# First-layer projection of a graph-attention block by one level of Strassen's scheme, logit rows kept in the result's last head

## The chip, the cores and the metric

One core of a Trainium2 chip runs the whole program as one launch. The metric is the device time of an execution in microseconds (us), less is better. Five engines work side by side, each through its own list of instructions in order: TensorE (PE, matrix products into PSUM; its weight loads are shown apart as PEld), VectorE (DVE), ScalarE (ACT), GpSimd (POOL) and SyncE (SP), which here issues most of the transfers (DMA). They wait for each other by semaphores: `wait_ge(sem, n)` stops an engine until `sem` has reached n, `then_inc` counts it up when an instruction is done.

## The reference, cut to what matters

The program is one transformer-like block for 1250 nodes of width 768: a layer norm, a two-layer graph attention network, a mixing layer, and a mixture of experts. The change touches the first graph layer:

```python
h = (x @ W).reshape(N, H, C)              # N 1250, x 768 wide, H 4 heads of C 512
al_s = einsum('nhc,hc->nh', h, a_src)
al_d = einsum('nhc,hc->nh', h, a_dst)
e = leaky_relu(al_s[src] + al_d[dst], 0.2)
m = segment_max(e, dst)                   # over the edges into a node
ex = exp(e - m[dst])
alpha = ex / (segment_sum(ex, dst)[dst] + 1e-16)
out = segment_sum(h[src] * alpha[:, :, None], dst)
```

All of it is float32. The edges have been counted earlier into a dense table of 1250 x 1250 counts, so that sums over edges become products with that table.

## The kernel before, in words

The phases follow each other with a barrier in between; the change lies in `first_layer_phase`, which computes three things at once.

**The projection** h = xn W. The normed input lies turned in SBUF as `xnT`, 6 blocks of 128 of its 768 features (KD = 6) by 1250 nodes. Nodes go in 10 tiles of 125 (NT, P), and W comes in 4 parts of 512 columns (C1), one for each head, into two buffers `w` in turn. A unit is one head and one tile: 6 float32 products of 125 nodes by 512 columns, summed up in one of two PSUM banks `G` (line 972), and copied by ScalarE into `h` (line 929). There are 40 units, head by head. Unit g waits until the copy of unit g - 2 is done.

**The attention logits**: 8 rows (4 heads, source and target side) from `wa`, as 3 x 6 products at the phase's start (line 978). ScalarE copies them to `alT` (line 951), SP stores them to DRAM and loads the four source rows back, spread over all partitions, as `rows` (line 862). TensorE also turns them (line 984) for `al`.

**The maxima**: for every tile t of target nodes, its counts are loaded (`ct`, lines 101 and 102), VectorE adds the self loop (line 898, function `loop`), ScalarE makes a mask of them (line 937), and VectorE takes for each of 4 heads the largest logit among the neighbours (line 914, 40 in all). TensorE turns the counts in ten blocks into a set of three PSUM banks `T` (line 996), ScalarE copies them to `co` (line 945), and GpSimd issues the stores of masks and counts for later phases. There are two sets `T`.

The order of each engine is written out by hand. TensorE: logits, unit 0, the turn of the logits, then units with the turn of tile t behind unit 3 + 2t, and the turn of the maxima (line 1004) behind unit 30. ScalarE copies each unit, and behind unit 3 + 2t the counts and then the mask of tile t + 2. VectorE has nothing to do with the products: it only does self loops and maxima. SP loads the counts of tile t when tile t - 2 has been turned and masked, the weights of head 2 behind the counts of tile 5, and those of head 3 last.

The next phase, `gat1_phase`, multiplies attention weights with `h` in halves of 256 columns (line 1188, into four banks `Z`).

Of the kernel before, what the change touches and what calls it, by code (L numbers as in the profile page):

```python
# [9 lines left out]
I32 = mybir.dt.int32  # L10
# [798 lines left out]
def first_layer_phase(nc, cx, W1, xnT, wa, ident, al, alT_dram, ct_dram, c_dram, mask_dram, mT_dram, h):  # L809
# [3 lines left out]
    MASK0, MAX_UNIT = 3, 30  # L813
    UNITS = H1 * NT
    J = 2 * H1
    gemm, h_evac, rows_done, rows_copied, al_turned, al_stored = (
        cx.sem("first_" + s) for s in ("gemm", "h_evac", "rows_done", "rows_copied", "al_turned", "al_stored"))
# [7 lines left out]
    dve_step = cx.sem("mask_step")  # L825
    with ExitStack() as st:
        w = [sb(nc, st, f"gnn_w1_{b}", [128, KD, C1]) for b in range(2)]
        alT = sb(nc, st, "logit_alT", [J, N])
# [3 lines left out]
        rows = sb(nc, st, "mask_rows", [128, H1, N])  # L832
# [4 lines left out]
        mT = sb(nc, st, "mask_mT", [H1, N])  # L837
        G = [pb(nc, st, f"first_G{b}", [P, C1]) for b in range(2)]
        T = [[pb(nc, st, f"mask_T{b}{j}", [128, 512]) for j in range(3)] for b in range(2)]
        width = [4, 4, 2]  # L840
        tiles = lambda bank, j, rows: bank[rows, 0:width[j] * P].rearrange("p (t d) -> p t d", d=P)
        block = st.enter_context(nc.Block())

        @block.sync
        def _(sp):
# [13 lines left out]
            sp.dma_start(alT_dram, alT[:]).then_inc(al_stored, 16)  # L859
# [3 lines left out]
            for t in range(2, NT):  # L863
                sp.wait_ge(turned, t - 1)
# [8 lines left out]
            sp.dma_start(mT_dram, mT[:]).then_inc(m_stored, 16)  # L873
# [3 lines left out]
        def _(pool):  # L877
            pool.memset(large[:], BIG).then_inc(consts, 1)
            pool.memset(h[:, :, :, C1:C1 + 1], 1.0)
            for t in range(NT):  # L880
# [4 lines left out]
                pool.dma_start(c_dram[t, :, :], co[b][:].rearrange("p t d -> p (t d)")).then_inc(c_stores[b], 16)  # L885
            for b in range(2):
                pool.wait_ge(mask_stores[b], 16 * (NT // 2))
                pool.wait_ge(c_stores[b], 16 * (NT // 2))

        @block.vector  # L890
        def _(dve):
# [7 lines left out]

            loop(0)  # L900
            loop(1)
            dve.wait_ge(al_turned, 1)
            step(dve.tensor_copy(al[:], T[1][0][0:P, 0:NT * J].rearrange("p (t j) -> p t j", j=J)))
            dve.wait_ge(rows_loaded, 64)
            for t in range(NT):
                b = t % 2
                if 1 <= t < NT - 1:
                    loop(t + 1)
                dve.wait_ge(masked, t + 1)
                for hd in range(H1):  # L910
                    n = H1 * t + hd
                    if n >= 1:
                        dve.wait_ge(maxed, n)
                    dve.tensor_tensor_reduce(out=junk[:], in0=rows[0:P, hd, :], in1=mk[b][:], scale=1.0,
                                             scalar=-3.0e38, op0=ALU.subtract, op1=ALU.max,
                                             accum_out=big[:, t, hd:hd + 1]).then_inc(maxed, 1)
            dve.wait_ge(maxed, H1 * NT)
            step(dve.tensor_tensor(big[:], big[:], al[:, :, H1:2 * H1], ALU.add))
            dve.scalar_tensor_tensor(m[:], big[:], SLOPE, big[:], ALU.mult, ALU.max).then_inc(m_ready, 1)
            for j in range(3):  # L920
                dve.wait_ge(m_turned, j + 1)
                dve.tensor_copy(mT[:, 4 * j * P:(4 * j + width[j]) * P], T[0][j][0:H1, 0:width[j] * P]
# [1410 lines left out]
```

## Time and profile before

| | us |
|---|---|
| median of 3 executions | 2211.65 (2207.43 to 2214.65) |
| the profiled execution, its own time | 2213.6 |
| its span | 2211.8 |
| TensorE busy in the span | 2084.3 (94%) |
| VectorE, ScalarE, GpSimd busy | 1107.5, 456.1, 199.3 |
| first-layer phase, from its first load to the next phase's first | 648.0 to 884.1 |

Times in the trace are counted from the start of the span. A busy time is the sum over an engine's instructions, without overlaps; an idle time is what stands before an instruction, with the one that ended it. A float32 product stands in the trace as two MATMUL rows, each with its own weight load, and a MATMUL row is longer than its distance to the next, since the end of one lies over the start of the next. The granted clock (PEclk) is a share of 2.4 GHz; it has the levels 1.00 and 0.50.

### The profile page before, as it was taken

To read this page: it belongs to the slowest core of one execution; us is meant where nothing else is said; L and a number is where in the kernel's file an instruction comes from. 1 tells how busy PE (TensorE), PEld (TensorE's weight loads), DVE (VectorE), ACT (ScalarE), POOL (GpSimd) and SP (SyncE) were. 2 spreads that over 40 slices of the span, in tenths; PEclk is the share of its full clock that TensorE was granted. 3 is DMA by queue.
4 is the path that set the end of the run, shared out by engine and by line. 5 is a ranking of instruction groups with operands and counts; after the bars stand their busy time and mean duration, and the time that the engine had idled before them with its cause. 6 is when DMAs were issued, how large, how long until landed. Compare 5 with 4: busy or idle time off the path is not lost. (4 is left out here: it accounts for less than half of the span.)

```text
span 2211.8 us, 32691 instructions
## 1 busy us (share of the span) xinstructions
PE 2084.3 (94%) x9768; PEld 1435.0 (65%) x9769; DVE 1107.5 (50%) x2517; ACT 456.1 (21%) x818; POOL 199.3 (9%) x187
## 2 busy tenths in 40 slices
PE   5999999999989999799999989998997999999997
PEld 3666566666644444688888745554664777777775
DVE  5766447662554510788888600306854343333343
ACT  2222221222002311122222200002432222222221
POOL 0000000000000000000000000001003233333232
PEclk9999999998999999899999989998995999999999
DMA  7000220002644510443333264424404888899654
GB/s 247 15 16 17 87 101 15 16 18 77 204 130 138 171 57 1 154 122 98 120 96 98 66 224 152 157 103 111 153 29 177 250 229 247 244 291 278 190 128 78
DMA packets 80954, 282.32 MB, mean 128 GB/s; under 512 B 11562, under 2 KB 32098, under 8 KB 71267
## 3 DMA queue, kind: packets, MB, share of 16 engines
q1 hardware_dynamic: 59858, 216.48, 29.2%
q0 software_dynamic: 14048, 51.06, 10.0%
q10 hardware_dynamic: 6960, 13.62, 1.8%
q8 instruction: 53, 0.87, 0.2%
q14 instruction: 35, 0.28, 0.0%
HBM read 222.26 MB, written 58.87 MB: 127 GB/s over the span
## 5 line engine op out<-in xcount | busy, mean ns | idle before, releaser
L1188 PE MATMUL gat_Z<-h,gat_wt 125*125 125x256 f32 (+1 forms) x1600 | 355.0, 381 | 17.8 <-DVE gat_wt L1104 17.8
L1188 PEld LDWEIGHTS gat_Z<-h,gat_wt 125*125 125x125 f32 x1600 | 298.2, 188 | 63.6 <-DVE gat_wt L1104 18.6
L732 PE MATMUL mix_G<-mix_w,xnT 128*125 128x384 f32 x720 | 243.8, 489 | 0.0
L1335 PE MATMUL gat2p_Y<-w_and_experts,gat2p_hT 128*125 128x386 f32 (+1 forms) x640 | 209.8, 490 | 10.2 <-DMA w_and_experts<-in_L_gnn_W 10.2
L972 PE MATMUL first_G<-gnn_w,xnT 128*125 128x512 f32 x480 | 208.3, 593 | 0.0
L732 PEld LDWEIGHTS mix_G<-mix_w,xnT 128*125 128x125 f32 x720 | 133.6, 190 | 85.6 <-issue 3.4
L1335 PEld LDWEIGHTS gat2p_Y<-w_and_experts,gat2p_hT 128*125 128x125 f32 x640 | 120.2, 188 | 98.5 <-issue 12.6
L972 PEld LDWEIGHTS first_G<-gnn_w,xnT 128*125 128x125 f32 x480 | 89.1, 188 | 110.4 <-issue 110.3
L1822 PE MATMUL gat_Z<-h,gat_wt 125*125 125x385 f32 (+1 forms) x400 | 135.7, 496 | 12.6 <-DVE gat_wt L1556 12.6
L1822 PEld LDWEIGHTS gat_Z<-h,gat_wt 125*125 125x125 f32 x400 | 74.8, 190 | 66.7 <-DVE gat_wt L1556 13.3
L639 DVE SCALAR_TENSOR_TENSOR mix_count_A<-count_ikey,count_off,keyT 128x512 f32 x120 | 90.2, 752 | 55.1 <-issue 46.9
L2059 DVE TENSOR_SCALAR ex_idS<-ex_ids 128x1 int32 x52 | 8.0, 154 | 214.1 <-DMA out_rows<-ex_y,ex_idS 214.1
L2147 PE MATMUL ex_PH<-ex_xT,w_and_experts 128*128 128x128 f32 x936 | 113.8, 282 | 1.5
L645 DVE TENSOR_SCALAR mix_count_B<-count_islo,sloT 128x314 f16 x480 | 112.1, 299 | 0.0
L2147 PE MATMUL ex_PH<-ex_xT,ex_w 128*128 128x128 f32 x936 | 111.0, 277 | 0.9 <-issue 0.3
L2147 PEld LDWEIGHTS ex_PH<-ex_xT,w_and_experts 128*128 128x128 f32 x936 | 109.2, 196 | 2.5 <-issue 2.2
L2157 PE MATMUL ex_PY<-ex_w,ex_hT 128*128 128x384 f32 x312 | 107.2, 493 | 0.9 <-ACT ex_hT L2088 0.9
L2157 PE MATMUL ex_PY<-w_and_experts,ex_hT 128*128 128x384 f32 x312 | 107.5, 494 | 0.5 <-ACT ex_hT L2088 0.5
L2147 PEld LDWEIGHTS ex_PH<-ex_xT,ex_w 128*128 128x128 f32 x936 | 106.5, 192 | 1.4 <-issue 1.4
L2004 POOL DMA_INDIRECT out_rows<-ex_y,ex_idS x52 | 82.6, 1588 | 271.3 <-DVE ex_y L2061 226.4
L2029 DVE SCALAR_TENSOR_TENSOR ex_Q<-posm,offs,ex_iota 125x1280 bf16<-125x1280 f32 x54 | 83.8, 1552 | 39.0 <-issue 39.0
L780 PE MATMUL mix_count_S<-mix_count_B,mix_count_A 128*128 x480 | 86.4, 297 | 5.2 <-issue 2.7
(310 smaller groups left out, 2490.7 us busy)
## 6 DMA issues: line engine op xcount, KB each, us to landing
w_and_experts<-in_L_ffn_W SPq DMA_DIRECT2D x32, 1152.0 KB
ex_w<-in_L_ffn_W SPq DMA_DIRECT2D x32, 1152.0 KB
gat_cnt<-c_dram SPq DMA_DIRECT2D x50, 546.9 KB
gat2p_hT<-h1T_dram SPq DMA_DIRECT2D x20, 1000.0 KB, 5.1
h1T_dram<-gat_oT ACTq DMA_DIRECT2D x40, 250.0 KB
mix_w<-in_L_mix_qkv_w SPq DMA_DIRECT2D x6, 1152.0 KB, 13.0
ct_dram<-mix_count_out SPq DMA_DIRECT2D x40, 157.0 KB, 2.1
mix_w_slice<-in_L_gnn_W SPq DMA_DIRECT2D x6, 1024.0 KB, 12.2
```

The lines of the kernel that those rows point to most:

```text
L639: dve.scalar_tensor_tensor(CA[:, bass.ds(s * RB, RB), :], ikey[:].unsqueeze(1).to_broadcast([128, RB, 128]), off[:, win:win + 1], keyT[:, ...
L645: last = dve.tensor_scalar(CB[:, bass.ds(s * RB + b, 1), :], islo[:].unsqueeze(1), sloT[:, bass.ds(r * RB + b, 1)], None, ALU.is_equal)
L732: last = pe.matmul(G[c][:], xnT[:, k, t * P:(t + 1) * P], w[:, k, c, :], start=(k == 0), stop=(k == KD - 1))
L780: last = pe.matmul(S[:], CA[:, bass.ds(s * RB + b, 1), :].rearrange("p o k -> p (o k)"), CB[:, bass.ds(s * RB + b, 1), :].rearrange("p o k ...
L972: last = pe.matmul(G[g % 2][:], xnT[:, k, t * P:(t + 1) * P], w[hd % 2][:, k, :], start=(k == 0), stop=(k == KD - 1))
L1188: last = pe.matmul(Z[b][j][:], wt[b][:, s, :], h[:, s, bass.ds(hd, 1), j * HC:(j + 1) * HC + j], start=(s == 0), stop=(s == NT - 1))
L1335: last = pe.matmul(Y[b][j][:, 0:HW if j else W], hT[q % 2][:, k, :], w[:, k, cols], start=(k == 0), stop=(k == KF - 1))
L1822: last = pe.matmul(Z[b][j][:], wt[b][:, s, :], h2[:, s, 385 * j:385 * j + CW[j]], start=(s == 0), stop=(s == NT - 1))
L2004: pool.indirect_dma_start(out, bass.IndirectOffsetOnAxis(ap=idS[:, 0:1], axis=0), y[:], None, compute_op=ALU.add).then_inc(added, 16)
L2029: dve.scalar_tensor_tensor(Q[:], posm[:, :, bass.ds(e, 1)].to_broadcast([P, NT, SLOT]), 1.0 if first else offs[:, bass.ds(at, 1)], iot[:]. ...
L2147: last = pe.matmul(PH[m][:], w1[b][:, k, m * 128:(m + 1) * 128], xT[:, k, :], start=(k == 0), stop=(k == KD - 1))
L2157: last = pe.matmul(PY[j][:], hT[:, k, :], w2[b][:, k, j * 384:(j + 1) * 384], start=(k == 0), stop=(k == KM - 1))
```

## The change

Nodes are split into two halves of 5 tiles (TOK = 625), features into two halves of 3 blocks (HK), the 512 columns of a head into two of 256 (HC). With the input's blocks A (nodes by features) and the weights' blocks B (features by columns), the four blocks of a head's result are got from seven block products where the plain way takes eight:

- sums of the input, once: S1 = A21 + A22 and S2 = S1 - A11 at the start, S3 = A11 - A21 (written over A21) and S4 = A12 - S2 when the logit products have read the input;
- sums of the weights for each head: B12 - B11, B22 - that, B22 - B12 (written over B12), B21 - the second;
- for a pair of tiles (t, t + 5) and a head, 20 pairs in all, each product being 3 float32 products of 256 columns: first A11 B11 and second A12 B21, whose sum is C11; sixth, seventh on top of first in its bank `X`; fifth, fourth, third in banks `Y5`, `Y4` and on top of fifth.

ScalarE copies the bank `X` into `h` three times a pair, after first, sixth and seventh. VectorE adds the banks `Y2`, `Y5`, `Y4`, `Y5` to what lies there (line 957 of the new code): C11, C22, C21, C12. The 40 maxima stand between these adds, three for each pair from pair 1 on, one behind C11 and two behind C21; the sums for the next head's weights stand behind C12. Tile t's counts are turned in pair 1 + 4t // 3, now into one set of three banks. The logit rows are spread into the place of head 3's result in `h`, which is free until pair 15; `alT` and `mT` lie in the buffer that the maxima write. `h` has its head outside its tile now, and some tables of earlier phases are freed sooner. Number and kind of the transfers stay.

```diff
-    MASK0, MAX_UNIT = 3, 30
-    UNITS = H1 * NT
+    HC, HK, HT = C1 // 2, KD // 2, NT // 2
+    PAIRS = H1 * HT
+    TOK = HT * P
+    MASK0, MAX_PER, MAX_PAIR, MT_PAIR = 1, 3, 16, 17
     J = 2 * H1
...
+    turn_pair = lambda t: MASK0 + 4 * t // MAX_PER
+    mask_pair = lambda t: MASK0 + (4 * (t - 2) + 3) // MAX_PER + 1
...
-        alT = sb(nc, st, "logit_alT", [J, N])
+        S1, S2, S4 = (sb(nc, st, f"first_S{i}", [128, HK, TOK]) for i in (1, 2, 4))
+        WT = [[sb(nc, st, f"first_W{b}{i}", [128, HK, HC]) for i in (1, 2, 4)] for b in range(2)]
...
+        alT, mT = junk[0:J, :], junk[0:H1, :]
+        rows = h[:, H1 - 1, :, :].rearrange("p t c -> p (t c)")[:, 0:H1 * N].rearrange("p (h n) -> p h n", n=N)
...
-        G = [pb(nc, st, f"first_G{b}", [P, C1]) for b in range(2)]
-        T = [[pb(nc, st, f"mask_T{b}{j}", [128, 512]) for j in range(3)] for b in range(2)]
+        X = [pb(nc, st, f"first_X{b}", [P, 512]) for b in range(2)]
+        Y2, Y5, Y4 = (pb(nc, st, f"first_Y{i}", [P, 512]) for i in (2, 5, 4))
+        T = [pb(nc, st, f"mask_T{j}", [128, 512]) for j in range(3)]
...
+        B = lambda hd, i, j: w[hd % 2][:, i * HK:(i + 1) * HK, j * HC:(j + 1) * HC]
+        S3 = xnT[:, 0:HK, TOK:N]
+        C = lambda n, i, j: h[0:P, n // HT, n % HT + i * HT, j * HC:(j + 1) * HC]
...
+                sp.wait_ge(turned, 3 * (t - 1))
                 sp.wait_ge(masked, t - 1)
                 load_counts(t)
                 if t == 5:
-                    sp.wait_ge(gemm, NT)
+                    sp.wait_ge(p3_done, HT)
                     load_w(2)
-            sp.wait_ge(gemm, 2 * NT)
+            sp.wait_ge(p3_done, 2 * HT)
             load_w(3)
...
+            pool.wait_ge(maxed, H1 * NT)
+            pool.memset(h[:, H1 - 1, :, C1:C1 + 1], 1.0)
...
+            def weight_sum(hd, i):
+                W = WT[hd % 2]
+                if i == 0:
+                    dve.wait_ge(w_loaded[hd % 2], 16 * (hd // 2 + 1))
+                    if hd >= 2:
+                        dve.wait_ge(p3_done, HT * (hd - 1))
+                    ins = dve.tensor_tensor(W[0][:], B(hd, 0, 1), B(hd, 0, 0), ALU.subtract)
+                elif i == 1:
+                    dve.wait_ge(t_ready, 4 * hd + 1)
+                    ins = dve.tensor_tensor(W[1][:], B(hd, 1, 1), W[0][:], ALU.subtract)
+                elif i == 2:
+                    ins = dve.tensor_tensor(B(hd, 0, 1), B(hd, 1, 1), B(hd, 0, 1), ALU.subtract)
+                else:
+                    dve.wait_ge(t_ready, 4 * hd + 2)
+                    ins = dve.tensor_tensor(W[2][:], B(hd, 1, 0), W[1][:], ALU.subtract)
+                ins.then_inc(t_ready, 1)
+
+            def largest(i):
+                t, hd = i // H1, i % H1
+                if hd == 0:
+                    if 1 <= t < NT - 1:
+                        loop(t + 1)
+                    dve.wait_ge(masked, t + 1)
...
+            def some_largest(n, part):
+                first = MAX_PER * (n - MASK0)
+                for i in range(first + part, first + (1 if part == 0 else MAX_PER)):
+                    if 0 <= i < H1 * NT:
+                        largest(i)
+
+            def tile_of(n, add, done, i, j, bank):
+                dve.wait_ge(done, n + 1)
+                if (i, j) != (1, 0):
+                    dve.wait_ge(x_kept, 3 * n + {(0, 0): 1, (1, 1): 3, (0, 1): 2}[i, j])
+                old = C(n, 1, 0) if (i, j) == (1, 1) else C(n, i, j)
+                dve.tensor_tensor(C(n, i, j), bank[:, 0:HC], old, ALU.add).then_inc(add, 1)
+
+            dve.tensor_tensor(S1[:], xnT[:, 0:HK, TOK:N], xnT[:, HK:KD, TOK:N], ALU.add).then_inc(s_ready, 1)
+            dve.wait_ge(s_ready, 1)
+            dve.tensor_tensor(S2[:], S1[:], xnT[:, 0:HK, 0:TOK], ALU.subtract).then_inc(s_ready, 1)
+            for i in range(4):
+                weight_sum(0, i)
             loop(0)
             loop(1)
+            dve.wait_ge(rows_done, CH)
+            dve.tensor_tensor(S3, xnT[:, 0:HK, 0:TOK], S3, ALU.subtract).then_inc(s_ready, 1)
+            dve.wait_ge(s_ready, 2)
+            dve.tensor_tensor(S4[:], xnT[:, HK:KD, 0:TOK], S2[:], ALU.subtract).then_inc(s_ready, 1)
             dve.wait_ge(al_turned, 1)
...
+            dve.tensor_copy(al[:], T[0][0:P, 0:NT * J].rearrange("p (t j) -> p t j", j=J)).then_inc(al_kept, 1)
+            for n in range(PAIRS):
+                hd, i = n // HT, n % HT
+                tile_of(n, c11, p2_done, 0, 0, Y2)
+                some_largest(n, 0)
+                tile_of(n, c22, p5_done, 1, 1, Y5)
+                dve.wait_ge(c22, n + 1)
+                tile_of(n, c21, p4_done, 1, 0, Y4)
+                some_largest(n, 1)
+                tile_of(n, c12, p3_done, 0, 1, Y5)
+                if i >= 1 and hd + 1 < H1:
+                    weight_sum(hd + 1, i - 1)
...
+            def keep(n, i, j, use):
+                act.wait_ge(x_done, 3 * n + use)
+                act.activation(C(n, i, j), X[n % 2][:, 0:HC], ACT.Copy).then_inc(x_kept, 1)
 
...
+            for n in range(PAIRS):
+                if n == HT * (H1 - 1):
+                    act.wait_ge(maxed, H1 * NT)
+                keep(n, 0, 0, 1)
+                for t in range(2, NT):
+                    if mask_pair(t) == n:
+                        make_mask(t)
+                keep(n, 0, 1, 2)
+                keep(n, 1, 0, 3)
+                for t in range(NT):
+                    if turn_pair(t) == n:
...
+            def product(bank, stationary, moving, fresh, done):
+                for k in range(HK):
+                    last = pe.matmul(bank[:, 0:HC], stationary(k), moving[:, k, :], start=fresh and k == 0,
+                                     stop=k == HK - 1, skip_group_check=True)
+                last.then_inc(done, 1)
+
+            def first(n):
+                hd, t = n // HT, n % HT
...
+                if n >= 2:
+                    pe.wait_ge(x_kept, 3 * (n - 1))
+                product(X[n % 2], lambda k: xnT[:, k, t * P:(t + 1) * P], B(hd, 0, 0), True, x_done)
+
+            def second(n):
+                hd, t = n // HT, n % HT
+                if n >= 1:
+                    pe.wait_ge(c11, n)
+                product(Y2, lambda k: xnT[:, HK + k, t * P:(t + 1) * P], B(hd, 1, 0), True, p2_done)
+
+            def sixth(n):
+                hd, t = n // HT, n % HT
+                if n == 0:
+                    pe.wait_ge(s_ready, 2)
+                pe.wait_ge(t_ready, 4 * hd + 2)
+                pe.wait_ge(x_kept, 3 * n + 1)
+                product(X[n % 2], lambda k: S2[:, k, t * P:(t + 1) * P], WT[hd % 2][1], False, x_done)
+
+            def fifth(n):
+                hd, t = n // HT, n % HT
+                if n >= 1:
+                    pe.wait_ge(c12, n)
+                product(Y5, lambda k: S1[:, k, t * P:(t + 1) * P], WT[hd % 2][0], True, p5_done)
+
+            def seventh(n):
+                hd, t = n // HT, n % HT
+                if n == 0:
+                    pe.wait_ge(s_ready, 3)
+                pe.wait_ge(t_ready, 4 * hd + 3)
+                pe.wait_ge(x_kept, 3 * n + 2)
+                product(X[n % 2], lambda k: S3[:, k, t * P:(t + 1) * P], B(hd, 0, 1), False, x_done)
+
+            def fourth(n):
+                hd, t = n // HT, n % HT
+                pe.wait_ge(t_ready, 4 * hd + 4)
+                if n >= 1:
+                    pe.wait_ge(c21, n)
+                product(Y4, lambda k: xnT[:, HK + k, (HT + t) * P:(HT + t + 1) * P], WT[hd % 2][2], True, p4_done)
+
+            def third(n):
+                hd, t = n // HT, n % HT
+                if n == 0:
+                    pe.wait_ge(s_ready, 4)
+                pe.wait_ge(c22, n + 1)
+                product(Y5, lambda k: S4[:, k, t * P:(t + 1) * P], B(hd, 1, 1), False, p3_done)
+
+            def turn(t):
+                pe.wait_ge(looped, t + 1)
+                if t == 0:
+                    pe.wait_ge(al_kept, 1)
+                else:
+                    pe.wait_ge(copied, t)
...
+            first(0)
+            second(0)
...
+            for n in range(PAIRS):
+                if n >= 1:
+                    second(n)
+                sixth(n)
+                fifth(n)
+                seventh(n)
+                fourth(n)
+                for t in range(NT):
+                    if turn_pair(t) == n:
+                        turn(t)
+                if n + 1 < PAIRS:
+                    first(n + 1)
+                third(n)
+                if n == MAX_PAIR:
...
-                                         h[:, s, bass.ds(hd, 1), j * HC:(j + 1) * HC + j],
+                                         h[0:P, bass.ds(hd, 1), s, j * HC:(j + 1) * HC + j],
...
-            h = sb(nc, st1, "h", [P, NT, H1, C1 + 1])
+            h = sb(nc, st1, "h", [128, H1, NT, C1 + 1])
```

On TensorE, before, units 2 to 4 and the turn of tile 0 in between. `first_G` is the unit's bank, `gnn_w1_0` the weights of head 0, `mask_T` the banks of a turn, `mask_ct` the counts; a row with x6 is one unit:

```order
L972 MATMUL first_G0<-gnn_w1_0,xnT 125x512 x6
L972 MATMUL first_G1<-gnn_w1_0,xnT 125x512 x6
L996 MATMUL mask_T00<-ident,mask_ct0 125x125 x4
L996 MATMUL mask_T01<-ident,mask_ct0 125x125 x4
L996 MATMUL mask_T02<-ident,mask_ct0 125x125 x2
L972 MATMUL first_G0<-gnn_w1_0,xnT 125x512 x6
```

On TensorE, now, pair 1 with the turn of tile 0 (second, sixth, fifth, seventh, fourth, the turn, first of pair 2, third). `first_W` and `first_S` are the sums:

```order
L1041 MATMUL first_Y2<-gnn_w1_0,xnT 125x256 x3
L1041 MATMUL first_X1<-first_W02,first_S2 125x256 x3
L1041 MATMUL first_Y5<-first_W01,first_S1 125x256 x3
L1041 MATMUL first_X1<-gnn_w1_0,xnT 125x256 x3
L1041 MATMUL first_Y4<-first_W04,xnT 125x256 x3
L1103 MATMUL mask_T0<-ident,mask_ct0 125x125 x4
L1103 MATMUL mask_T1<-ident,mask_ct0 125x125 x4
L1103 MATMUL mask_T2<-ident,mask_ct0 125x125 x2
L1041 MATMUL first_X0<-gnn_w1_0,xnT 125x256 x3
L1041 MATMUL first_Y5<-gnn_w1_0,first_S4 125x256 x3
```

Where one unit of six stood, products of three into alternating banks stand, and the bank `X` of a pair is written three times with other work between.

On VectorE, before, the maxima of tile 1 behind the self loop of tile 2. `mask_mk` is the mask, `mask_big` takes the maxima (its 125x1 row reads out what the row ahead summed up):

```order
L898 TENSOR_TENSOR mask_ct0<-mask_ct0,ident 125x125
L914 ISA mask_junk,mask_big<-mask_rows,mask_mk1 125x1250
L914 ISA mask_big 125x1
L914 ISA mask_junk,mask_big<-mask_rows,mask_mk1 125x1250
L914 ISA mask_big 125x1
```

On VectorE, now, the end of pair 2 and the start of pair 3: the self loop of tile 2, two maxima, C12, a weight sum of head 1, C11, one maximum, C22, C21:

```order
L913 TENSOR_TENSOR mask_ct0<-mask_ct0,ident 125x125
L942 ISA mask_junk,mask_big<-h,mask_mk1 125x1250
L942 ISA mask_big 125x1
L942 ISA mask_junk,mask_big<-h,mask_mk1 125x1250
L942 ISA mask_big 125x1
L957 TENSOR_TENSOR h<-first_Y5,h 125x256
L924 TENSOR_TENSOR first_W12<-gnn_w1_1,first_W11 128x768
L957 TENSOR_TENSOR h<-first_Y2,h 125x256
L942 ISA mask_junk,mask_big<-h,mask_mk1 125x1250
L942 ISA mask_big 125x1
L957 TENSOR_TENSOR h<-first_Y5,h 125x256
L957 TENSOR_TENSOR h<-first_Y4,h 125x256
```

Between the maxima stand adds for which TensorE waits, and they wait for TensorE.

## Rows read from the trace of the kernel before

**Rows 1.** Windows: busy us of PE, PEld, DVE, ACT, POOL; granted clock; DMA share; GB/s.
```profile
650.00:652.00 2.00, 2.00 (x4) 0.40 (x3) 0.00 (x0) 0.00 (x0) 0.00 (x0) 0.50 0.94 339
663.00:883.00 220.00, 219.62 (x601) 102.79 (x600) 62.57 (x94) 49.78 (x81) 10.87 (x20) 1.00 0.29 92
730.00:732.00 2.00, 2.00 (x13) 1.47 (x12) 1.76 (x4) 0.68 (x2) 0.00 (x0) 1.00 0.55 210
905.00:1265.00 360.00, 360.00 (x1742) 312.06 (x1741) 305.32 (x387) 91.14 (x116) 0.00 (x0) 1.00 0.32 99
```
**Rows 2.** Groups by shape, 647 to 895: count, busy us, mean ns, idle before.
```profile
L972 PE MATMUL first_G<-gnn_w,xnT 128*125 128x512 f32 x480 | 208.3, 593 | 0.0
L972 PEld LDWEIGHTS first_G<-gnn_w,xnT 128*125 128x125 f32 x480 | 89.1, 188 | 110.4 <-issue 110.3
L996 PE MATMUL mask_T<-ident,mask_ct 125*125 125x125 f32 x100 | 12.5, 272 | 0.0
...
L945 ACT ACTIVATE mask_co<-mask_T 125x250 f32<-125x250 f32 x10 | 3.9, 388 | 0.0
```
**Rows 3.** Order of time, TensorE, end of the projection: start, us, merged instructions.
```profile
836.11 46.52 PE L972 MATMUL first_G<-gnn_w,xnT 128*125 128x512 f32 x108
```
**Rows 4.** Order of time, TensorE, a piece of the next stage.
```profile
947.87 8.82 PE L1188 MATMUL gat_Z<-h,gat_wt 125*125 125x256 f32 x40
956.52 0.59 PE L1198 MATMUL gat_T<-ident,gat_o 125*128 125x125 f32 x4
```
**Rows 5.** The page's costliest groups: that stage's products.
```profile
L1188 PE MATMUL gat_Z<-h,gat_wt 125*125 125x256 f32 (+1 forms) x1600 | 355.0, 381 | 17.8 <-DVE gat_wt L1104 17.8
```
**Rows 6.** Order of time: unit 0, logit turn, unit 1 on, loads at unit 2.
```profile
662.98 5.42 PE L972 MATMUL first_G<-gnn_w,xnT 128*125 128x512 f32 x12
...
667.37 0.19 PEld L972 LDWEIGHTS first_G<-gnn_w,xnT 128*125 128x125 f32 x1 [0.24 <-issue]
668.32 1.16 PEld L984 LDWEIGHTS mask_T<-ident,logit_alT 8*125 8x125 f32 x10 [0.76 <-issue]
...
669.50 15.71 PE L972 MATMUL first_G<-gnn_w,xnT 128*125 128x512 f32 x36
...
674.76 0.19 PEld L972 LDWEIGHTS first_G<-gnn_w,xnT 128*125 128x125 f32 x1 [0.24 <-issue]
...
675.18 0.19 PEld L972 LDWEIGHTS first_G<-gnn_w,xnT 128*125 128x125 f32 x1 [0.24 <-issue]
```
**Rows 7.** Groups by shape, VectorE, whole span.
```profile
L1092 DVE TENSOR_TENSOR gat_u<-al,gat_rows 125x1250 f32<-125x1250 f32 x40 | 58.2, 1455 | 55.2 <-DMA gat_rows<-mT_dram 55.2
...
L1115 DVE SCALAR_TENSOR_TENSOR gat_o<-gat_Z,gat_rden,gat_brow 125x256 f32<-125x256 f32 x40 | 19.0, 475 | 0.0
...
L510 DVE TENSOR_TENSOR proj_x<-proj_Y,proj_x 125x384 f32<-125x384 f32 x20 | 11.2, 558 | 30.0 <-PE proj_Y L474 29.7
...
L505 DVE TENSOR_TENSOR proj_x<-proj_x,proj_bias 125x768 f32<-125x768 f32 x10 | 9.5, 953 | 0.0
```
**Rows 8.** Order of time, 640 to 700: self loop, masks, first maxima.
```profile
659.74 0.29 DVE L898 TENSOR_TENSOR mask_ct<-mask_ct,ident 125x125 f32<-125x125 f32 x1 [2.18 <-DMA mask_ct<-ct_dram]
...
663.50 2.55 ACT L937 ACTIVATE mask_mk<-mask_ct,mask_large 125x1250 bf16<-125x1250 f32 x2
...
676.04 1.46 DVE L914 CUSTOM_DVE_ANT_0 mask_junk<-mask_rows,mask_mk 125x1250 f32<-125x1250 f32 x1 [6.19 <-DMA mask_rows<-alT_dram]
...
677.55 1.46 DVE L914 CUSTOM_DVE_ANT_0 mask_junk<-mask_rows,mask_mk 125x1250 f32<-125x1250 f32 x1
```
**Rows 9.** Order of time, SP: issues of tile 5's counts and head 2's weights.
```profile
720.52 0.30 SPq L101 DMA_DIRECT2D mask_ct<-ct_dram  x1
...
721.31 0.40 SPq L847 DMA_DIRECT2D gnn_w<-in_L_gnn_W  x1
```
**Rows 10.** Order of time, weight loads of the logit products, [idle before], early and later.
```profile
651.41 0.13 PEld L978 LDWEIGHTS mask_T<-xnT,gnn_wa 128*8 128x8 f32 x1 [0.56 <-issue]
...
653.44 0.09 PEld L978 LDWEIGHTS mask_T<-xnT,gnn_wa 128*8 128x8 f32 x1 [0.26 <-issue]
```

More of the change, by code:

```diff
@@ L878, in _ @@
             pool.memset(large[:], BIG).then_inc(consts, 1)
-            pool.memset(h[:, :, :, C1:C1 + 1], 1.0)
+            pool.memset(h[:, 0:H1 - 1, :, C1:C1 + 1], 1.0)
             for t in range(NT):
@@ L902, in _ @@
+            dve.tensor_tensor(S4[:], xnT[:, HK:KD, 0:TOK], S2[:], ALU.subtract).then_inc(s_ready, 1)
             dve.wait_ge(al_turned, 1)
[L903 to L922, printed above, removed]
-                                ).then_inc(m_copied, 1)
+            dve.tensor_copy(al[:], T[0][0:P, 0:NT * J].rearrange("p (t j) -> p t j", j=J)).then_inc(al_kept, 1)
@@ new lines, in _ @@
+            for n in range(PAIRS):
[9 more added lines that the diff above has]
+                    weight_sum(hd + 1, i - 1)
+                if n == MAX_PAIR - 1:
+                    dve.wait_ge(maxed, H1 * NT)
+                    dve.wait_ge(al_kept, 1)
+                    step(dve.tensor_tensor(big[:], big[:], al[:, :, H1:2 * H1], ALU.add))
+                    dve.scalar_tensor_tensor(m[:], big[:], SLOPE, big[:], ALU.mult, ALU.max).then_inc(m_ready, 1)
+                if n == MT_PAIR:
+                    for j in range(3):
+                        dve.wait_ge(m_turned, j + 1)
+                        dve.tensor_copy(mT[:, 4 * j * P:(4 * j + width[j]) * P], T[j][0:H1, 0:width[j] * P]
+                                        ).then_inc(m_copied, 1)
@@ L944, in keep_counts @@
                 for j in range(3):
-                    last = act.activation(co[b][:, 4 * j:4 * j + width[j], :], tiles(T[b][j], j, slice(0, P)), ACT.Copy)
+                    act.wait_ge(turned, 3 * t + j + 1)
+                    last = act.activation(co[b][:, 4 * j:4 * j + width[j], :], tiles(T[j], j, slice(0, P)), ACT.Copy)
                 last.then_inc(copied, 1)
@@ L954, in _ @@
             make_mask(1)
-            for g in range(UNITS):
-                keep_h(g)
-                t = (g - MASK0) // 2
-                if g >= MASK0 and (g - MASK0) % 2 == 0 and t < NT:
-                    keep_counts(t)
-                    if t + 2 < NT:
-                        make_mask(t + 2)
+            for n in range(PAIRS):
[9 more added lines that the diff above has]
+                    if turn_pair(t) == n:
+                        keep_counts(t)
@@ L967, in unit @@
                 if t == 0:
                     pe.wait_ge(w_loaded[hd % 2], 16 * (hd // 2 + 1))
-                if g >= 2:
-                    pe.wait_ge(h_evac, g - 1)
-                for k in range(KD):
-                    last = pe.matmul(G[g % 2][:], xnT[:, k, t * P:(t + 1) * P], w[hd % 2][:, k, :],
-                                     start=(k == 0), stop=(k == KD - 1))
-                last.then_inc(gemm, 1)
+                if n >= 2:
+                    pe.wait_ge(x_kept, 3 * (n - 1))
@@ new lines, in turn @@
+            def turn(t):
+                pe.wait_ge(looped, t + 1)
+                if t == 0:
+                    pe.wait_ge(al_kept, 1)
+                else:
+                    pe.wait_ge(copied, t)
+                for j in range(3):
+                    for s in range(4 * j, 4 * j + width[j]):
+                        last = pe.transpose(T[j][0:P, s % 4 * P:(s % 4 + 1) * P], ct[t % 2][:, s * P:(s + 1) * P],
+                                            ident[0:P, 0:P])
+                    last.then_inc(turned, 1)
```

58 lines of the change are left out of this document (22 added, 36 removed).

## Prediction

> **What bounds the kernel now.** I read the busy time by stage first. From the first product to the end of the projection TensorE is busy 219.6 of 220 us at a granted clock of 1.00, which is the level of 2.4 GHz, while VectorE works 62.6 us and ScalarE 49.8 us of it [rows 1]. So this stage is as long as its row of TensorE instructions, and the next stage begins when it ends; the chain of waits on the page reaches back only to the last stage and says nothing here. Second, the instructions grouped by line and shape: every float32 product stands in the trace as two passes, so 240 products of 512 columns are 480 passes [rows 2]. The reader is to see that a busy group of 208.3 us is almost all of the 219.6, and that its weight loads (188 ns each) fit beside passes more than twice as long. Third, the order of time: 108 passes in 46.52 us, of which 0.16 is the tail of the last (a pass is shown 592 ns long and the next starts earlier). That is 0.4292 us from start to start [rows 3], and 480 of them are 206.0 us. The other 13.6 us are the turns of logits, counts and maxima, which the change keeps.
>
> **The change part by part.**
>
> *The products.* Seven products of half width, 3 float32 products each, for 20 pairs of tiles are 420, or 840 passes of 256 columns. The trace has such passes already, in the next stage, which also is busy without a gap at 1.00 [rows 1]: 40 passes of 256 and 257 columns from 947.87 to the start of the turn at 956.52, 8.65 us, or 0.2163 each [rows 4]. Their weight loads, as wide as those here, stay hidden. 840 times 0.2163 is 181.7 us. Against 206.0 that is **24.3 us less**. Bounds: half of 0.4292 is 0.2146, giving 180.3 and 25.7 less; the mean over that whole group is 355.0 us over 1600 passes, 0.2219 [rows 5], giving 186.4 and 19.6 less. I take 0.2163, since it is read in an unbroken row.
>
> *Waits at the borders.* Before there were 40 units with one wait each, now 140 products with one to three. The wait of unit 2 on the copy of unit 0 leaves no mark: loads at 674.76 and 675.18 stand as far apart as any [rows 6]. A wait that is fulfilled early costs nothing there. So the question is which waits are fulfilled early. One pair without a turn, from the start of its second product, with 6 x 0.2163 = 1.30 us for each product: second 0, sixth 1.30, fifth 2.60, seventh 3.89, fourth 5.19, first of the next pair 6.49, third 7.79, end 9.08. A result is there 0.16 after its product (381 ns shown for a pass against 216 between starts) [rows 4, 5]. A ScalarE copy of 250 columns takes 0.388 [rows 2]; I take 0.39 for 256. An add from PSUM and SBUF lies between its nearest rows, 0.475 for 256 columns with one operand more and 0.558 for 384 [rows 7]; I take 0.48. Then:
> - seventh needs the copy behind sixth: 2.76 + 0.39 = 3.15, and is due at 3.89. Slack 0.74.
> - third needs the add into C22, which needs seventh's copy: 5.35 + 0.39 + 0.48 = 6.22, due 7.79. Slack 1.57.
> - fifth of the next pair needs the add into C12. On VectorE that add is queued behind the add into C21 (done 6.65 + 0.48 = 7.13) and two of the maxima, 1.51 from start to start [rows 8], so until 10.15; it ends at 10.63, and fifth is due at 9.08 + 2.60 = 11.68. Slack 1.05. Behind it stand a weight sum and the next pair's adds.
> Per pair VectorE has 4 x 0.48 + 3 x 1.51 + 0.95 = 7.4 us of work in 9.08. In the six pairs where adding the self loop falls between the maxima TensorE has a turn as well (12.5 us for ten [rows 2]), 1.25 us more room. ScalarE's mask (two in 2.55 [rows 8]) and copy of counts fit between its copies. Turning into one set of three banks instead of two waits for the copy of the turn before, at least a whole pair earlier. I price all of this at 0; taken all by itself, 0.1 us lost in each pair would be 2 us.
>
> *The sums in front.* S1 and S2 are 1875 columns; 768 take 0.953 and 1250 take 1.455 [rows 7], so 2.1 us each. They run from 648 to 652.3 under the logit products. The four sums of head 0's weights (0.95 each) wait for that load, which is issued ahead of the counts that land before 659.74 [rows 8]; even from 657 they end at 661, ahead of the masks at 663.50. Then S3 and S4, 4.2 us, to 667.2. TensorE meanwhile does two products and the logit turn (its old distance, from 662.98 + 12 x 0.4292 = 668.13 to 669.50, 1.37 us [rows 6]): 662.98 + 2.60 + 1.37 = 666.95, where sixth wants the copy that ScalarE makes behind both masks, at 666.05 + 0.39 = 666.44. Seventh wants S3 at 669.5, third S4 at 673.4. Cover holds; if it were gone, 4.2 us is the whole price. The sums for later heads stand last in VectorE's row of a pair.
>
> *Loads.* The logit rows go to another place by the same four transfers; they landed at 676.04 [rows 8]. The first maximum now stands behind the add into C11 of pair 1, which starts at 666.95 + 6 x 1.30 = 674.7; the add ends at 674.7 + 1.30 + 0.16 + 0.48 = 676.7. Head 2's weights, issued at 721.31, were in by 732, when the transfers ebb [rows 1, 9]; in the new order they are issued in pair 5 at 6.49 + 1.25 (turn) + 0.8 = 8.5 of 10.33 us, and the first sum of them stands behind the add into C12 at the end of pair 6, 10.33 + 0.16 + 0.48 = 10.97 after its start: 12.8 us later, where 11 were needed. Behind that sum the chain to third of pair 7 (0.95 + 0.48 + 1.51 + 0.48 = 3.4, due at 7.79) leaves 3.7 us more. The layout of h leaves the next stage runs of 256 columns as before. 0.
>
> *The sum.* 2213.6 (the profiled execution; span 2211.8) - 24.3 = 2189.3. That execution lies 2.0 above the median of the three runs; 2187.3 on the median. I predict **2188**, between them.
>
> **Rivals.**
> *Every border costs something.* The trace has one border with a gap: the last first_G load at 667.37 belongs to a pass that ends at 668.13, the logit turn loads at 668.32 [rows 6]. Such 0.19 us at each of the 100 borders that are new would be 19 us: 2189.3 + 19 = 2208, no difference. For it: a product is now over after six short passes. Against it: that gap stands before a stationary operand of another shape (8 rows), the others show none. It decides from 0.18 us a border.
>
> *Part of the slack is eaten.* If the copy behind sixth came 1.1 us later than I have it (a mask in front of it that waits for the last maximum), seventh would wait 0.36 us in each pair. If an add cost 1.0 rather than 0.48, VectorE's own row would be 9.48 us a pair against 9.08. Either is some 0.4 us in each of 20 pairs: 8 us, 2197. For it: slack of 0.74 is half a product. Against it: only eight pairs have a mask, and no row of this size comes near 1.0.
>
> *The clock falls: slower.* At the start of this stage the trace shows the logit passes 0.69 us apart (a load of 0.13 and 0.56 before it) at a granted 0.50, which is 1.2 GHz, and 0.35 for such passes later: a pass costs twice [rows 1, 10]. If the product borders made TensorE idle so often that a third of the 840 passes fell to that level, 280 x 0.2163 = 60.6 us come on top: 2250. It decides from 113 passes, 24.3 / 0.2163. Against it: the next stage goes through four banks in groups of 20 passes, and shows 1.00 over 360 us [rows 1].
> The Trainium skill, "TensorE: Matmul & The Clock Gate", section "A second HAM failure mode: psum-queue depth-cycling", has this rule: cycling through PSUM banks makes the engine idle briefly between groups of matmuls, so that its clock goes up and down. By that rule the time would be this rival's; the row of the next stage does not agree with it, though its groups are longer than six passes.
>
> *Half-width passes don't pay.* If weight load and pass did not overlap, a pass would be 0.188 + 0.216 = 0.404 us, 339 us in all, 133 slower. It decides from 0.245 a pass. The next stage has this very ratio and shows 0.2163 [rows 4].
>
> **How the numbers follow.** Forecast 0.74; part of the slack 0.12; border gaps 0.07; clock 0.04; no overlap 0.03. The forecast's own range is 2213.6 - 25.7 = 2187.9 to 2194.0 by the two prices of a pass, less the 2.0 to the median and widened below by the runs' own spread of 4: 2181 to 2194. To leave out no more than 2 in 10 the range goes up past the 2197 of partial stalls: 2180 to 2201. This kernel's measurement can tell about 0.3%, 6.6 us. Faster takes the first two cases but for a little of the second: 0.84. Same is the border case and that little: 0.09. Slower is the clock and the missing overlap: 0.07.
>
> **What would show it.** Right: weight loads of the products 0.216 us apart across borders, TensorE without a gap over a stage of about 195 us (219.6 - 24.3) at 1.00; ScalarE copies near 0.39 and VectorE adds below 0.5; the turn of the maxima and the store behind it done before the stage ends. Wrong: idle time of TensorE put down to the ScalarE copies (behind sixth) or to VectorE adds of C12; loads further apart at borders alone; a granted clock under 1.00 inside the stage; a first sixth or seventh product that starts after 667 or 669.5; or a next stage with another length than its 360 us.

## The result, and the profile after

The changed kernel runs in 2188.8 us (median of 5 executions, 2179.17 to 2192.41) against 2207.43 before (5, 2205.44 to 2214.65). The ratio is 0.9895, with a 95% interval of 0.987 to 0.992, which is 23.2 us of 2207.43; the two medians alone lie 18.6 us apart. A second comparison on another occasion gave 0.9886 (0.9864 to 0.9907). So it is faster, by about 1%, and the forecast of 2188 holds.

What is best compared is the **stretch** from the first product of the projection to the end of its last, since it hardly varies (196.38 us in both profiled executions of the changed kernel): 663.0 to 882.59 before, 219.59 us, and 656.80 to 853.18 after, 196.38 us. Below is this window of each kernel (its length; busy us of PE, PEld, DVE, ACT, POOL; granted clock, DMA share, GB/s), to be read beside [rows 1]. Before and after:

```profile
663.00:882.59 219.59, 219.59 (x601) 102.79 (x600) 62.57 (x94) 49.44 (x80) 10.87 (x20) 1.00 0.29 92
```
```profile
656.80:853.18 196.38, 195.46 (x961) 170.13 (x960) 106.97 (x187) 49.06 (x101) 11.03 (x21) 1.00 0.33 105
```

TensorE has 960 rows where it had 600 and needs 23.2 us less, still at 1.00. Its weight loads now fill 170 of 196 us, and VectorE works 107 us where it worked 63. The page's first part after, and the stage's instructions in groups by shape (count, busy us, mean ns, idle before), to be read beside [rows 2, 7]:

```profile
PE 2053.4 (94%) x10128; PEld 1499.2 (69%) x10129; DVE 1159.5 (53%) x2617; ACT 454.5 (21%) x838; POOL 201.5 (9%) x188
```
```profile
L1041 PE MATMUL first_X<-gnn_w,xnT 128*125 128x256 f32 x240 | 58.6, 380 | 0.9 <-ACT h L998 0.9
L942 DVE CUSTOM_DVE_ANT_0 mask_junk<-h,mask_mk 125x1250 f32<-125x1250 f32 x40 | 58.2, 1455 | 0.3
...
L957 DVE TENSOR_TENSOR h<-first_Y,h 125x256 f32<-125x256 f32 x80 | 33.9, 424 | 88.8 <-ACT h L998 58.6 <-PE first_Y L1041 29.8
...
L998 ACT ACTIVATE h<-first_X 125x256 f32<-125x256 f32 x60 | 23.0, 383 | 124.1 <-PE first_X L1041 124.1
```

An add takes 0.424 us, a copy 0.383. VectorE waits 88.8 us ahead of its adds, TensorE only 0.9 us in all, put down to ScalarE's copy. Those 0.9 us are two gaps, in pairs 5 and 9 (pairs are counted from 0). The order of time shows where the first comes from (start, us, instruction, [idle before <- who ended it]; L957 is an add, L929 a weight sum, L913 the self loop, L1006 the mask, L998 a copy; 709.51 is sixth, 710.81 fifth, 712.72 seventh; weight loads are left out):

```profile
709.12 0.42 DVE L957 TENSOR_TENSOR h<-first_Y,h 125x256 f32<-125x256 f32 x1
709.45 0.95 DVE L929 TENSOR_TENSOR first_W<-gnn_w,first_W 128x768 f32<-128x768 f32 x1
709.51 1.46 PE L1041 MATMUL first_X<-first_W,first_S 128*125 128x256 f32 x6
710.32 0.42 DVE L957 TENSOR_TENSOR h<-first_Y,h 125x256 f32<-125x256 f32 x1
710.65 0.28 DVE L913 TENSOR_TENSOR mask_ct<-mask_ct,ident 125x125 f32<-125x125 f32 x1
710.81 1.46 PE L1041 MATMUL first_Y<-first_W,first_S 128*125 128x256 f32 x6
...
710.97 1.34 ACT L1006 ACTIVATE mask_mk<-mask_ct,mask_large 125x1250 bf16<-125x1250 f32 x1 [3.46 <-DVE mask_ct L913]
712.21 0.36 ACT L998 ACTIVATE h<-first_X 125x256 f32<-125x256 f32 x1
...
712.72 1.53 PE L1041 MATMUL first_X<-gnn_w,xnT 128*125 128x256 f32 x6 [0.46 <-ACT h L998]
714.09 1.46 PE L1041 MATMUL first_Y<-first_W,xnT 128*125 128x256 f32 x6
```

Products start 1.295 us apart, but seventh comes 1.91 after fifth. ScalarE's copy of sixth was ready to start at 710.97 and stood behind a mask; the mask waited for the self loop; and the self loop stands on VectorE behind C12 of the pair before, a weight sum and C11.

The profiled execution after has a span 29.1 us shorter (2182.7 against 2211.8), 5.9 more than the stretch gives. That part lies ahead of the stretch, which starts 6.2 us earlier, and the start varies by more than this from one execution to another: see the last section.

### The profile page after: what moved, and what is told of

Read it like the earlier page. It is cut to its first block and busy times, and to the rows that moved or that the text cites. A ratio compares the mean times of both kernels' runs of the same rounds, so it can differ in the third digit from the quotient of the medians.

```text
span 2182.7 us, 33677 instructions
## 1 busy us (share of the span) xinstructions
PE 2053.4 (94%) x10128; PEld 1499.2 (69%) x10129; DVE 1159.5 (53%) x2617; ACT 454.5 (21%) x838; POOL 201.5 (9%) x188
## 5 line engine op out<-in xcount | busy, mean ns | idle before, releaser
L2228 ACT ACTIVATE ex_y<-ex_PY,ex_gate 128x384 f32<-128x384 f32 x52 | 30.2, 580 | 286.6 <-DMA out_rows<-ex_y,ex_idS 248.9
L2289 PEld LDWEIGHTS ex_PY<-ex_w,ex_hT 128*128 128x128 f32 x312 | 57.2, 190 | 39.3 <-ACT ex_hT L2220 2.3
```

The source lines that it names most:

```text
L2228: act.activation(y[:, 384:768], PY[1][:], ACT.Copy, scale=gate[:, slot]).then_inc(y_a, 1)
L2289: last = pe.matmul(PY[j][:], hT[:, k, :], w2[b][:, k, j * 384:(j + 1) * 384], start=(k == 0), stop=(k == KM - 1))
```

## The experiments

Each is told by its stretch, beside 196.38 of the changed kernel and 219.59 of before. Where no ratio is given the kernel was executed once, and only its stretch is used.

**Half width, all eight products.** The kernel before, with a unit done as two halves:

```diff
-                for k in range(KD):
-                    last = pe.matmul(G[g % 2][:], xnT[:, k, t * P:(t + 1) * P], w[hd % 2][:, k, :], ...)
+                for j in range(2):
+                    half = slice(j * C1 // 2, (j + 1) * C1 // 2)
+                    for k in range(KD):
+                        last = pe.matmul(G[g % 2][:, half], xnT[:, k, t * P:(t + 1) * P], w[hd % 2][:, k, half], ...)
```

> The kernel before, with each unit of 512 columns done as two halves of 256: all eight block products, 960 passes of 256 columns instead of 480 of 512. My theory (a pass costs its columns, 0.2159 us, and the gain is the eighth product left out): 960 x 0.2159 = 207.3 us against 206.0, so the stretch from the first product to the end of the last goes from 219.6 to 220.9 us, and the time does not differ from before (ratio 1.000 to 1.002). Rival, half width is itself worse or better: at 0.2219 a pass 213 us, a stretch of 227 and a ratio of 1.003; at anything under 0.2146 a stretch under 219.

```profile
658.90:879.68 220.78, 220.78 (x1081) 192.85 (x1080) 62.58 (x94) 49.43 (x80) 10.86 (x20) 1.00 0.29 93
```

220.78 us, ratio 0.9997 (0.9985 to 1.001). Its last 216 passes stand in one unbroken row:

```profile
832.92 46.79 PE L974 MATMUL first_G<-gnn_w,xnT 128*125 128x256 f32 x216
```

(46.79 - 0.16) / 216 = 0.2159 us, as expected. Half width alone costs 1.2 us here and gains nothing; the whole gain is the 120 passes that are left out: 120 x 0.2159 = 25.9, less these 1.2 and the 1.4 of the two gaps (see below), is 23.3, and 23.2 were measured.

**The second product twice.** The changed kernel, with eight products a pair again:

```diff
+                for k in range(HK):
+                    pe.matmul(Y2[:, 0:HC], xnT[:, HK + k, t * P:(t + 1) * P], B(hd, 1, 0)[:, k, :], start=k == 0, ...)
                 product(Y2, lambda k: xnT[:, HK + k, t * P:(t + 1) * P], B(hd, 1, 0), True, p2_done)
```

> The changed kernel, with the second product of each pair computed twice in the same place: eight products a pair again, all else as changed. My theory (the row of passes sets the stage): 20 x 1.295 = 25.9 us more, the stretch of 196.3 us becomes 222.2, at a granted clock of 1.00. Rival, the stage is set by VectorE's or ScalarE's queue and TensorE waits for it: less than 20 us more.

```profile
663.70:884.68 220.98, 220.98 (x1081) 192.61 (x1080) 107.42 (x187) 49.06 (x101) 11.03 (x21) 1.00 0.28 92
```

24.6 us more, 1.3 less than expected, and TensorE is busy without a gap. The passes cost what they should (20 x 1.295 = 25.9), and the two gaps are gone: each pair leaves VectorE 1.3 us more, and seventh of pair 5 starts 1.32 us after fifth where it was 1.91. So TensorE's row sets the stage, and the gaps belong to a short pair.

**More waits.** The changed kernel with 280 waits more that are long fulfilled:

```diff
                 for k in range(HK):
+                    if k >= 1:
+                        pe.wait_ge(rows_done, CH)
```

> The changed kernel, with a wait that has long been fulfilled ahead of the second and the third matmul of every product, 280 more waits on TensorE. My theory (a fulfilled wait costs nothing): the stretch stays at 196.3 us, within 0.5. Rival, a border costs 0.19 us each: up to 53 us more, 249.

```profile
655.70:852.08 196.38, 195.42 (x961) 170.19 (x960) 106.96 (x188) 49.07 (x101) 11.04 (x21) 1.00 0.33 105
```

196.38 us, to the hundredth what it was. A fulfilled wait costs TensorE nothing. With that, and with no idle time in the trace after at any border but the two of pairs 5 and 9, the rival of the border gaps falls.

**Tight order.** The same products without other work between those that share a bank `X`; ScalarE's mask goes behind its third copy as well, which these lines leave out:

```diff
-                if n >= 1:
-                    second(n)
                 sixth(n)
-                fifth(n)
                 seventh(n)
+                if n >= 1:
+                    second(n)
+                fifth(n)
                 fourth(n)
...
-                if n + 1 < PAIRS:
-                    first(n + 1)
                 third(n)
+                if n + 1 < PAIRS:
+                    first(n + 1)
```

> The changed kernel with the same products in a tight order: first, sixth, seventh directly behind each other, then second, fifth, fourth, third (the mask goes behind ScalarE's third copy, since the order needs it). Sixth and seventh now each wait for ScalarE's copy: 0.16 until the result, 0.38 for the copy and some 0.1 of hand-offs, 0.65 to 0.7 us twice in each of 20 pairs, 26 to 28 us. My theory: a stretch of 196.3 - 1.2 + 27 = 222 us, the gain gone (ratio about 1.00), with a granted clock that stays at 1.00. Rival, such short stops make the clock fall: a granted clock under 1.00 in the stretch and more than 235 us.

```profile
660.00:885.48 225.48, 203.89 (x961) 167.17 (x960) 105.23 (x187) 49.35 (x101) 11.04 (x21) 1.00 0.29 90
```
```profile
PE first_X L1041 <- ACT h L998: 21.6, 38, 0.6
```
```profile
706.62 1.46 PE L1041 MATMUL first_X<-gnn_w,xnT 128*125 128x256 f32 x6
...
708.11 0.39 ACT L998 ACTIVATE h<-first_X 125x256 f32<-125x256 f32 x1 [1.85 <-PE first_X L1041]
...
708.64 1.53 PE L1041 MATMUL first_X<-first_W,first_S 128*125 128x256 f32 x6 [0.57 <-ACT h L998]
710.74 1.53 PE L1041 MATMUL first_X<-gnn_w,xnT 128*125 128x256 f32 x6 [0.57 <-ACT h L998]
712.10 1.46 PE L1041 MATMUL first_Y<-gnn_w,xnT 128*125 128x256 f32 x6
```

225.48 us, 3.5 over the 222 that I gave, ratio 1.0038 (1.0022 to 1.0055): with the same seven products the kernel is slower than before. A stop is shown as 0.57 us idle but costs 2.02 - 1.295 = 0.73 and 2.10 - 1.295 = 0.81 from start to start. Against the kernel without gaps below (194.98) it is 30.5 us over 38 stops, 0.80 each. I had 0.65 to 0.70, with 0.16 until the result, 0.38 for the copy and some 0.1 of hand-offs. The trace has 0.20 (706.62 + 1.295 to 708.11), 0.39, and 0.14 from the copy's end to the next pass (708.50 to 708.64); and a product behind a stop takes 1.36 us from its start to the next (710.74 to 712.10), 0.07 more than others. The clock stays at 1.00 through all of them, so the rival on the clock does not hold for stops of this length.

**The changed kernel again, and the mask later.** The second has ScalarE's mask behind the copy that seventh needs:

```diff
                 keep(n, 0, 0, 1)
-                for t in range(2, NT):
-                    if mask_pair(t) == n:
-                        make_mask(t)
                 keep(n, 0, 1, 2)
+                for t in range(2, NT):
+                    if mask_pair(t) == n:
+                        make_mask(t)
                 keep(n, 1, 0, 3)
```

> The changed kernel once more, beside the next one on the same chip: a stretch of 196.3 us from the first product to the end of the last, a gap of 0.6 us ahead of seventh in pairs 5 and 9, and a time about 23 us under before (ratio near 0.9895). Its times and granted clock ahead of the stretch may differ from run to run by some us.

> The changed kernel with ScalarE's mask behind the second copy of a pair instead of in front of it. My theory (in pairs 5 and 9 the mask waits for a self loop that VectorE does behind C11 of the same pair, and the copy that seventh needs is queued behind it): both gaps of 0.62 us go, the stretch is 195.1 us, 1.2 shorter; the time cannot tell that from the changed kernel. Rival, the gap comes from VectorE alone or moves to third, whose add waits for the third copy: a stretch still at 196.3 or more.

```profile
661.60:857.98 196.38, 195.43 (x961) 170.10 (x960) 106.97 (x187) 49.07 (x101) 11.03 (x21) 1.00 0.32 103
```
```profile
660.30:855.28 194.98, 194.98 (x961) 170.25 (x960) 106.98 (x187) 49.08 (x101) 11.03 (x21) 1.00 0.34 105
```

The changed kernel repeats its 196.38 exactly (ratio 0.9886, 0.9864 to 0.9907). With the mask later TensorE is busy for the whole stretch, 194.98 us, 1.4 less. The chain through the mask is thus shown as the cause of both gaps. Its ratio of 0.989 (0.987 to 0.9911) can't be told from the changed kernel's; it is the better stretch, not a faster time that could be measured.

**More work on VectorE.** An extra sum into a spare tile behind each of the four adds of a pair, of 256 columns (small) or 800 (large):

```diff
                 dve.tensor_tensor(C(n, i, j), bank[:, 0:HC], old, ALU.add).then_inc(add, 1)
+                if doses[0]:
+                    dve.wait_ge(dosed, doses[0])
+                doses[0] += 1
+                flat = S1[0:P].rearrange("p k n -> p (k n)")
+                dve.tensor_tensor(dose[:], flat[:, 0:W], flat[:, W:2 * W], ALU.add).then_inc(dosed, 1)   # W 256 or 800
```

> The changed kernel with an extra VectorE instruction of about 0.42 us behind each of the four adds of a pair (a sum of 256 columns into a spare tile). By my timetable VectorE's row goes from 7.2 to 8.9 us a pair against 9.07, and the add into C12 still ends before fifth needs it: no gap in general, only the two gaps of pairs 5 and 9 grow by 0.4 each, a stretch of 196.3 to 198 us. Rival, VectorE has less room than that: 0.5 us in each pair with maxima, 203 us or more.

> The same with a sum of 800 columns, about 1.0 us, behind each add. VectorE's row is then 11.2 us a pair where it has maxima and weight sums: 13 x (4 x 1.42 + 4.5) + 12 x 0.95 + 8 x 0.28 = 146 us over pairs 1 to 13, where TensorE needs 13 x 9.07 + 12.5 = 130.4. My theory: VectorE becomes the bound there, 12 to 22 us more, a stretch of 208 to 218, with TensorE's gaps ahead of fifth, put down to the adds. Rival, the adds are not on the path at all: a stretch under 200.

Small:

```profile
665.30:863.98 198.68, 195.64 (x961) 170.09 (x960) 131.77 (x267) 49.06 (x101) 11.03 (x21) 1.00 0.32 102
```
```profile
722.15 1.53 PE L1047 MATMUL first_X<-gnn_w,xnT 128*125 128x256 f32 x6 [1.47 <-ACT h L1004]
763.39 1.53 PE L1047 MATMUL first_X<-gnn_w,xnT 128*125 128x256 f32 x6 [1.46 <-ACT h L1004]
```

Large:

```profile
658.30:865.28 206.98, 199.86 (x961) 172.30 (x960) 173.37 (x266) 49.48 (x101) 11.07 (x21) 0.98 0.32 100
```
```profile
717.39 1.54 PE L1047 MATMUL first_X<-gnn_w,xnT 128*125 128x256 f32 x6 [3.37 <-ACT h L1004]
762.49 2.26 PE L1047 MATMUL first_X<-gnn_w,xnT 128*125 128x256 f32 x6 [3.37 <-ACT h L1004]
802.92 1.56 PE L1047 MATMUL first_Y<-first_W,first_S 128*125 128x256 f32 x6 [0.25 <-DVE h L958]
```

The small sums cost 2.3 us, a little over the range that I gave. 2.0 of it stands in the same two gaps, which grow by 1.0 each and not by 0.4: the chain of that gap has three sums in it (behind C21 and C12 of the pair before, and behind C11), each worth 0.33 from start to start. The large ones cost 10.6 us, under the 12 to 22 that I gave, and not where I said: 6.7 of 7 us of idle time are those two gaps again, and only one wait ahead of fifth is put down to an add. My sum was also too high because it added up shown durations. In the queue an add takes 0.34 us from its start to the next start (0.42 shown), a large sum 0.89 (0.98 shown), so pairs 1 to 13 need 134.7 us of VectorE and not 146, against 130.4 of TensorE.

And here the clock falls. Windows behind the first gap of 3.37 us (714.02 to 717.39; the clock is the third number from the right), then TensorE's rows behind both gaps:

```profile
717.30:718.70 1.40, 1.30 (x6) 1.19 (x7) 0.00 (x0) 0.00 (x0) 0.00 (x0) 1.00 0.00 0
718.70:720.00 1.30, 1.30 (x5) 1.00 (x4) 0.54 (x2) 0.39 (x1) 0.00 (x0) 0.53 0.00 0
720.00:722.00 2.00, 2.00 (x8) 1.69 (x7) 1.18 (x3) 0.00 (x0) 0.00 (x0) 0.50 0.00 0
722.00:724.00 2.00, 2.00 (x14) 1.86 (x14) 2.00 (x3) 1.34 (x3) 0.00 (x0) 0.95 0.11 15
```

```profile
718.76 2.74 PE L1047 MATMUL first_Y<-first_W,xnT 128*125 128x256 f32 x6
721.29 1.69 PE L1109 MATMUL mask_T<-ident,mask_ct 125*125 125x125 f32 x10
722.82 1.46 PE L1047 MATMUL first_X<-gnn_w,xnT 128*125 128x256 f32 x6
...
764.54 2.46 PE L1047 MATMUL first_Y<-first_W,xnT 128*125 128x256 f32 x6
766.84 1.25 PE L1109 MATMUL mask_T<-ident,mask_ct 125*125 125x125 f32 x10
```

One product after the gap at 1.00, then some 3 us at 0.50, which is 1.2 GHz. Behind the second gap it falls within the first product (762.49, six passes in 2.05 us). By the starts, fourth takes 2.53 and 2.30 us behind the two gaps instead of 1.295, the turn behind the first 1.53 instead of 1.09, and seventh behind the second 2.05 instead of 1.37: 3.4 us of the 10.6.

**Large sums and the mask later.** That leaves open whether VectorE was too full or the chain too long. Both edits together:

> The extra VectorE sum of 800 columns behind each add, together with ScalarE's mask behind the second copy of a pair. My theory now (of the 10.6 us that the sums cost, nearly all went through one chain: the self loop of pairs 5 and 9 late on VectorE, the mask behind it, the copy behind that, and the fall of the clock after these two gaps): the two gaps and the fall go, TensorE has only small gaps ahead of fifth near the end of the maxima, where VectorE's row is fullest (by distances from start to start 13 x (4 x 1.23 + 4.5) + 12 x 0.87 + 8 x 0.22 = 134.7 us against 130.4): a stretch of 195 to 199 us at a granted 1.00. Rival, VectorE is simply too full with these sums: 205 us or more, with gaps spread over the pairs.

```profile
658.60:856.08 197.48, 196.59 (x961) 169.82 (x960) 172.89 (x266) 48.86 (x101) 11.03 (x21) 1.00 0.33 103
```
```profile
PE first_Y L1047 <- DVE h L958: 0.8, 3, 0.3
```

197.48 us at 1.00. With VectorE busy 172.9 us instead of 107.0 the stretch is 2.5 us longer than with the mask later alone (194.98). So of the 10.6 us that the sums cost, 2.5 stay and 8.1 hang on the mask's place and the clock behind it; moving the mask is worth 9.5 us with these sums and 1.4 without. What stays is VectorE's own: three short waits ahead of fifth are shown (0.8 us), and by the starts fifth is late in five pairs (5, 6, 9, 10 and 13), which with the longer product behind makes 2.3 of the 2.5.

## Why the prediction was right

- **Products.** 24.3 us were forecast, 23.2 measured on the stretch. A pass takes 0.2159 us where 0.2163 was taken from the next stage, 0.3 us more gain in all; the 1.4 us of the next point take it to 23.2. That the gain is 1/8 of the passes and nothing else is shown by the half-width kernel and by the second product done twice.
- **Waits at the borders.** Right in that fulfilled waits cost nothing (shown), and wrong in one place. "ScalarE's mask (two in 2.55 [rows 8]) and copy of counts fit between its copies": in pairs 5 and 9 the mask does not, since its self loop stands behind C11 of the same pair. I had looked at the six pairs in which the self loop falls between two maxima and not at the two in which it stands ahead of the first. Measured: 1.4 us for both, where the prediction put 0; its own sign of being wrong, idle time put down to the copy behind sixth, shows there and nowhere else. The rival of eaten slack had named most of this mechanism (a mask in front of the copy, though one that waits for the last maximum and not for the self loop), priced at 0.36 in 20 pairs; it was 0.6 to 0.7 in two.
- **Sizes.** Adds 0.424 for 0.48, copies 0.383 for 0.39. The hand-offs that I left out cost 0.14 from copy to product, as the tight order shows, so the slack of seventh was nearer 0.5 than 0.74. It held.
- **The sums in front.** S1 to S4 take 2.10 to 2.11 each (2.1 said). Sixth of pair 0 starts 3.96 us after the first product; 3.97 was forecast. Head 0's weights were in at 649.56, 6.8 us after their issue, and the sums done before the masks. The cover held, and was not tried without.
- **Loads.** No wait for rows or weights stands in the stretch. That head 2's weights were in by 732 was read from a DMA share of 0.55 in [rows 1], which does not show it: the share is 1.01 again at 734 to 736. The term came to 0 all the same. The next stage is as long as before: 364.6 us (900.4 to 1265.0) against 364.0 (871.1 to 1235.1).
- **The clock.** 1.00 throughout: cycling through five banks in groups of six passes left no idle time but the two gaps of 0.46 us, and even 38 stops of 0.57 us did not move the granted clock. Stops of 3.37 us did. The rule of the Trainium skill that I weighed ("TensorE: Matmul & The Clock Gate", "A second HAM failure mode: psum-queue depth-cycling") does not show in the changed kernel's trace: neither the idle times between groups nor a fall of the clock.
- **The place of the logit rows, the single set of turn banks.** No effect shows in the trace after; neither was undone by itself.

The sum holds by its mechanism, as the stretch shows: 24.3 against 23.2. That the total came out within a us is luck. The forecast took its 24.3 from one execution of 2213.6 us and settled between that and the median of three, 2211.65; from the median of five, 2207.43, the same sum gives 2183.1, 5.7 under the measured 2188.8, and single executions of the changed kernel lie 13 us apart.

## What to carry to other kernels

Where one engine's row of instructions sets a stage, work taken off it is worth its full time as long as each wait of that engine is fulfilled before it gets there: here the order of the seven products was worth 30 us, more than the eighth product (26). Check each queue for the one chain in which several engines wait for each other within a short pair, not only the average room: VectorE took 66 us more for 2.5 us, while with the mask in a wrong place the same load cost 10.6. And compare a stretch of the trace, not only the total, when the total varies by as much as the effect.

## What the runs showed of the hardware

At a granted 1.00 a float32 pass costs its columns: 0.4292 us for 512, 0.2159 for 256, with weight loads of 0.188 hidden behind either, even when they fill 170 of 196 us.

The total varies with the granted clock ahead of the stage. The instructions ahead of it are the same in all kernels here, though three small tables lie elsewhere in the changed ones; yet the stretch starts between 655.7 and 665.3 us in eleven profiled executions, and at 656.8 and 661.6 in two of the same kernel. The mean granted clock up to that start goes with it: 0.98 in the five that start by 658.9, 0.97 in the five from 660.0 to 663.7, 0.96 in the one at 665.3. One place is seen in the mixing layer, before and after, windows and one group of products:

```profile
510.00:520.00 10.00, 7.38 (x23) 5.36 (x23) 1.03 (x2) 1.20 (x3) 0.00 (x0) 0.50 0.20 52
520.00:530.00 10.00, 10.00 (x32) 5.62 (x31) 0.00 (x0) 5.96 (x12) 0.00 (x0) 0.85 1.03 347
...
512.31 3.73 PE L760 MATMUL mix_KV<-mix_vs,mix_phik 125*128 125x97 f32 x16 [0.69 <-ACT mix_phik L720]
```
```profile
510.00:520.00 10.00, 7.41 (x28) 4.59 (x27) 1.03 (x2) 2.50 (x5) 0.00 (x0) 0.83 0.51 172
520.00:530.00 10.00, 10.00 (x61) 7.59 (x60) 1.27 (x5) 4.31 (x9) 0.00 (x0) 1.00 0.79 235
...
510.94 2.03 PE L760 MATMUL mix_KV<-mix_vs,mix_phik 125*128 125x97 f32 x16 [0.69 <-ACT mix_phik L720]
```

The first window stands at 0.50 in one and at 0.83 in the other, and the same sixteen products took 3.73 us and 2.03. Why the clock falls there in some executions and not in others was not tried.

On VectorE a shown duration overstates what an instruction takes from the queue: adds shown as 0.42 us start 0.34 apart from their successors, sums shown as 0.98 start 0.89 apart.
